# First attention of a two-layer model: single PSUM banks in rings of three, the shift and the value products placed at other steps, loops written out

## The reference

```python
x = x + delta_rule_attention(layernorm(x))     # layer 0
x = x + attention_and_experts(layernorm(x))    # layer 0: 16 heads of width 8, then 8 experts
x = x + attention(layernorm(x))                # layer 1: 32 heads of width 32
x = x + fourier_filter(layernorm(x))           # layer 1
```

```python
q, k, v = hn @ wq + bq, hn @ wk + bk, hn @ wv + bv     # 16 heads of width 8
scores = einsum('bhqd,bhkd->bhqk', q, k) / sqrt(8)
attn = softmax(scores, axis=-1)
o = einsum('bhqk,bhkd->bhqd', attn, v)
x = x + (o @ wo + bo)
```

## Time and profile before

| | us |
|---|---|
| Median of three runs | 2202.83 |
| The runs | 2204.41, 2199.51, 2202.83 |
| The profiled execution | 2194.15 |
| Its span, from the first to the last instruction | 2192.4 |

### The profile page before, as it was taken

How to read it: one execution, slowest core, us unless ns; L and a number is a source line. 1 busy time by engine, 2 the same in 40 slices (tenths; PEclk the granted TensorE clock), 3 DMA queues, 4 the chain that set the end, 5 groups by cost and what they waited for, 6 DMA issues and landing times. The chain is left out here.

```text
span 2192.4 us, 49876 instructions
## 1 busy us (share of the span) xinstructions
PE 1866.6 (85%) x18758; PEld 864.7 (39%) x18758; DVE 1681.2 (77%) x2951; ACT 1244.5 (57%) x2377; POOL 1132.9 (52%) x683
## 2 busy tenths in 40 slices
PE   5457753899999965897998999999999999999975
PEld 3357631122322224573442344444444444444433
DVE  8832565787878728444655999999999999999947
ACT  5312142677777740124773677777777777777755
POOL 8622641000000007331110788888888888888868
PEclk9778766799999985898997999999999999999995
DMA  1220046111111114116777333222323222333201
GB/s 45 48 31 3 0 124 182 35 36 43 35 35 42 29 48 132 47 50 230 285 304 239 79 79 78 70 70 78 79 79 79 74 71 72 79 79 79 64 10 40
DMA packets 198304, 179.84 MB, mean 82 GB/s; under 512 B 59508, under 2 KB 161012, under 8 KB 197892
## 3 DMA queue, kind: packets, MB, share of 16 engines
q1 hardware_dynamic: 189700, 170.02, 27.1%
q0 software_dynamic: 2944, 7.10, 1.1%
q10 hardware_dynamic: 5504, 0.73, 0.2%
HBM read 101.16 MB, written 75.26 MB: 80 GB/s over the span
## 5 line engine op out<-in xcount | busy, mean ns | idle before, releaser
L892 POOL TENSOR_TENSOR part_sums_l<-probs_l 128x1024 f32<-128x1024 f32 x256 | 610.3, 2384 | 214.4 <-ACT probs_l L957 203.9
L957 ACT ACTIVATE probs_l<-exp_l 128x512 f32<-128x512 f32 x1024 | 573.6, 596 | 166.4 <-PE exp_l L1005 148.7
L916 DVE TENSOR_REDUCE maxima_l<-max_l 128x1 f32<-128x512 f32 x1024 | 643.9, 679 | 4.3 <-PE max_l L994 1.5
L994 PE MATMUL max_l<-k_stack_l,q_stack_l 96*128 96x512 f16 x1024 | 400.0, 391 | 12.2 <-DVE pv_bank_l L908 10.3
L1005 PE MATMUL exp_l<-q_stack_l,k_stack_l 100*128 100x512 f16 x1024 | 389.7, 381 | 2.0 <-ACT probs_l L957 1.6
L1210 DVE TENSOR_REDUCE maxima_l<-max_l 128x2 f32<-128x1024 f32 x256 | 305.7, 1223 | 79.7 <-PE max_l L1293 78.4
L1246 ACT ACTIVATE probs_l<-exp_l 128x512 f32<-128x512 f32 x512 | 282.8, 598 | 117.1 <-PE exp_l L1307 116.3
L1039 PE MATMUL pv_bank_l<-probs_l,v_ring_l 128*32 128x512 f32 x2048 | 272.7, 605 | 0.3 <-issue 0.3
L1715 POOL IOTA rows_e<- 128x32 int32 x1 | 0.2, 184 | 455.2 <-POOLq L26 455.2
L994 PEld LDWEIGHTS max_l<-k_stack_l,q_stack_l 96*128 96x128 f16 x1024 | 99.7, 97 | 289.3 <-DVE maxima_l L916 216.7
L898 POOL TENSOR_TENSOR part_sums_l<-part_sums_l 128x512 f32<-128x512 f32 x128 | 184.1, 1438 | 10.0
(11 more groups left out here) (278 smaller groups left out, 2561.2 us busy)
## 6 DMA issues: line engine op xcount, KB each, us to landing
scratch_qk_l<-parts_g SPq DMA_DIRECT2D x128, 256.0 KB, 2.7
q_stack_l<-scratch_qk_l SPq DMA_DIRECT2D x192, 128.0 KB, 2.9
k_stack_l<-scratch_qk_l SPq DMA_DIRECT2D x192, 128.0 KB, 3.0
scratch_v_l<-v_g SPq DMA_DIRECT2D x16, 1024.0 KB
v_ring_l<-scratch_v_l SPq DMA_DIRECT2D x64, 256.0 KB, 3.4
scratch_stack_l<-parts_c SPq DMA_DIRECT2D x96, 128.0 KB, 2.4
q_stack_l<-scratch_stack_l SPq DMA_DIRECT2D x64, 96.0 KB, 2.1
k_stack_l<-scratch_stack_l SPq DMA_DIRECT2D x64, 96.0 KB, 2.1
```

Of the source, the lines that this page charges most:

```text
L892: pool.tensor_tensor(part_sums[:, i, h, :, :], probs[:, i, h, 0:2, :], probs[:, i, h, 2:4, :], ALU.add).then_inc(pair_sum.sem, 1)
L916: dve.reduce_max(maxima[:, s % 2, at % NT, at // NT:at // NT + 1], max_bank(n, at)[:, :], AX).then_inc(max_taken.sem, 1)
L957: act.activation(probs[:, i, at // NT, at % NT, :], exp_ps[at % 2][:, :], ACT.Exp, scale=a.scale).then_inc(prob_tile.sem, 1)
L994: pe.matmul(max_bank(n, at)[:, :], qs[0:SHIFT_ROW, s % RING, h, k * P:(k + 1) * P], ks[0:SHIFT_ROW, s % RING, h, :], start=True, stop=True ...
```

## The change

It touches `attention_l0` alone.

- PSUM: the two pairs `max_ps` become three single banks, and `exp_ps` gets three instead of two. Tile `at` of group `n` uses bank `(n * TILES + at) % 3` in either ring, and PE waits for the tile three before.
- DVE reduces each tile by itself: 16 reductions of 128 x 512 in a group instead of 8 of 128 x 1024.
- ACT makes `shift` after tile 4 instead of tile 6 (`L0_SHIFT_AT`). It copies `pv_bank` after tile 0 instead of tile 1 (`L0_COPY_AT`).
- The pieces of the values move (`L0_VALUES_AT`): two at step 1, one each at 2, 3 and 4, two at step 5, one at 6, none at 7. Before, there was one at each of steps 1 to 7, with two at step 3.
- The loops are gone: every engine's program of this stage is written out, and waits on constants.

The core of the diff:

```diff
-PV_PIECES = {1: (0,), 2: (1,), 3: (2, 3), 4: (4,), 5: (5,), 6: (6,), 7: (7,)}
...
+L0_MAXT_AT, L0_SHIFT_AT, L0_COPY_AT = 2, 4, 0
+L0_VALUES_AT = (1, 1, 2, 3, 4, 5, 5, 6)
+L0_VALUEST_AT, L0_INVERSE_AT = 4, 4
+L0_OT_AT, L0_OUT_AT = 7, 7
...
-        max_ps, exp_ps = [pb(f"max{i}", HALVES, N) for i in range(2)], [pb(f"exp{i}", N) for i in range(HALVES)]
+        max_ps, exp_ps = [pb(f"max{i}", N) for i in range(3)], [pb(f"exp{i}", N) for i in range(3)]
...
+        def bank(n, at):
+
+            return (n * TILES + at) % 3
...
-                        dve.wait_ge(max_pair.sem, max_pair.made(n, p))
-                        dve.reduce_max(maxima[:, s % 2, :, k, hh], max_ps[p % 2][:, :, :], AX).then_inc(max_taken.sem, 1)
...
+                        for half in range(HALVES):
+                            at = HALVES * p + half
+                            dve.wait_ge(max_tile.sem, max_tile.made(n, at))
+                            dve.reduce_max(maxima[:, s % 2, half, k, hh:hh + 1], max_ps[bank(n, at)][:, :], AX).then_inc(max_taken.sem, 1)
...
-                        if at == 6 and exists(turn, s, 1):
+                        if at == L0_COPY_AT and exists(turn, s, OUT_LAG):
+                            act.wait_ge(pv_ps.sem, pv_ps.made(n - OUT_LAG, 0))
+                            if exists(turn, s, OUT_LAG + 1):
+
+                                act.wait_ge(pvT_ps.sem, pvT_ps.made(n - OUT_LAG - 1, 0))
+                            act.copy(pv[:, :], pv_bank[:, :]).then_inc(pv_sb.sem, 1)
+                        if at == L0_SHIFT_AT and exists(turn, s, 1):
...
-                    if p == 0 and exists(turn, s, OUT_LAG):
-                        act.wait_ge(pv_ps.sem, pv_ps.made(n - OUT_LAG, 0))
-                        if exists(turn, s, OUT_LAG + 1):
-
-                            act.wait_ge(pvT_ps.sem, pvT_ps.made(n - OUT_LAG - 1, 0))
-                        act.copy(pv[:, :], pv_bank[:, :]).then_inc(pv_sb.sem, 1)
-
-            stream(act, step)
+
+            for n in range(M + OUT_LAG + 3):
+                step(n // U, n % U)
...
-                        if p >= 2:
-                            pe.wait_ge(max_taken.sem, max_taken.made(n, p - 2))
...
+                            at = HALVES * p + half
+                            if at >= 3:
+                                pe.wait_ge(max_taken.sem, max_taken.made(n, at - 3))
...
-                            if p:
-                                pe.wait_ge(prob_tile.sem, prob_tile.made(m, at - HALVES))
+                            if at >= 3:
+                                pe.wait_ge(prob_tile.sem, prob_tile.made(m, at - 3))
...
-                        for piece in PV_PIECES[p]:
+                        for piece in [piece for piece in range(2 * NT) if L0_VALUES_AT[piece] == p]:
```

## The result

The changed kernel takes 2132.62 us, the median of four runs (2129.23 to 2134.26), against 2201.17 us for the kernel before in the same comparison (2198.28 to 2204.41). The medians lie 68.5 us apart, 3.1%. The ratio of the two kernels is estimated as 0.9695, with a 95% interval from 0.9678 to 0.9713; it is not the quotient of these two medians, which is 0.9689. Between the two profiled executions the difference is 59.9 us (2194.15 to 2134.26). The profiled execution of the kernel before, which all sums are made against, was 7.0 us under its median, that of the changed kernel 1.6 us over its own.

What follows compares the result with a forecast made beforehand. Bound: the PE-ACT-PE-ACT-SP-PE chain over the shift's DMAs. 31 turns of 10.7 (331.7), 4 for `wo` and 14 for the clock make 350 instead of 397 us: 47 off 2202.83 gives 2156, range 2140 to 2184.

Steps and rivals of the forecast that it cites:

- The old bound and the length of the new chain: First exp product through shift and DMAs to the next: 12.02 us before, 10.55 after, 1.47 less; chance as bound 0.60.
- The lag: From the shift's end over SP's eight DMAs to the next first exp product: 6.53 us, unchanged.
- The plain turn: Turn of the first attention's stage without the product by `wo`: 10.7 us, ends 10.3 and 11.6.
- DVE takes over: Rival: reductions at 0.68 us make DVE the bound, 11.6 us a group; 29 us less, 2174; chance 0.16.
- The turn with `wo`: One turn in four, with the product by `wo`: 0.5 us over the plain one; 4 us for eight turns.
- PE takes over: Rival: paired max products no longer run together, 12.2 us of PE a turn; 5 us less, 2198; chance 0.07.
- The clock: PE's clock in the stage: falls stay, ten instead of eighteen assumed, costing 14 us in the sum.
- the two rivals with more falls or a slower clock: Falls in every turn: 20 us less, 2183, chance 0.10. PE at 1.2 GHz throughout: 160 us more, chance 0.05.
- The third exp bank: PE's exp-product waits at steps 0 and 1: zero by itself; without it the copy's 0.48 us could be lost.
- The loops: Writing out the stage's programs: counted as zero; register work at most 0.1 us a turn, 3 us in all.
- The pieces: Value products moved off step 7, leaving it to the product with `wo`; a double piece holds PE 0.98 us.
- The median: Whole kernel's time: 47 us taken off the median of 2202.83, giving 2156.

Runs made afterwards that it cites:

- e4: Changed kernel with the shift back after tile 6 and the copy back after tile 1; 2216.91 us, ratio to the kernel before 1.0085.
- e8: Changed kernel with DVE taking the maximum of only the first 256 of 512 columns of each tile; 2122.06 us, ratio 0.9649.
- e11: Changed kernel with the shift alone back after tile 6, the copy staying after tile 0; 2183.48 us, ratio 0.9925.
- e1: Kernel before with the loops of the first attention written out, nothing else changed; 2195.61 us, ratio 0.9989.
- e2: Kernel before with loops written out, shift after tile 4 and copy after tile 0, banks and pieces as before; 2195.64 us, ratio 0.9991.
- e3: Kernel before with PE making the max products of steps 0 and 1 three times over; 2189.87 us, ratio 0.9959.
- e5: Changed kernel with two banks for the exponentials instead of three; 2201.04 us, ratio 1.0006.
- e7: Kernel before with loops written out, shift and copy sooner and pieces as changed, banks as before; 2203.33 us, ratio 1.0023.
- e12: Kernel before with loops written out, shift and copy sooner, and max products of step 1 made three times over; 2183.41 us, ratio 0.9923.
- e10: Changed kernel measured once more, in another series; 2135.87 us, ratio 0.9712.
- e6: Changed kernel with the pieces of the values placed as before; 2139.55 us, ratio 0.9728.

## Why the prediction was right and wrong

**The old bound and the length of the new chain: right.** Every step from the first exp product to the end of the shift came within 0.15 us of the forecast, the end of the shift within 0.02. e4, e8 and e11, in which this chain is the bound, have turns of its length plus 6.36 to 6.38. The lag I had at 6.53; it is 6.36 to 6.38 in e1 already, so the difference came with the loops, written out on all engines at once. What was wrong is that the cut of the chain would count in full: e2 shows the next limit just behind it.

**The plain turn: right in size (10.7 forecast, 10.74 measured), wrong in what sets it.** I had the DMA chain as the bound at 10.55 and DVE 0.4 us behind. It is DVE, at 10.74, with the chain at 10.38 (e8). DVE's own work is 10.1 us, sixteen reductions 0.60 apart and 0.49 for the division, where I had 10.2. The other 0.66 are lost where PE is late with a max product: 0.28 twice and 0.1 once. I had expected 0.1 to 0.3 us of this, so that the size of 10.7 came out is in part luck. The reductions are 0.60 apart, not 0.68, so the rival "DVE takes over" came true in its mechanism and not at its price. The turn with `wo` is 0.75 over the plain one, where I had 0.5. Without the clock my sum was 335.7 and the stage is 338.45. In the rival "PE takes over" the sum holds a 0.53 that no row gives; with the 0.44 that it names for a pair apart it would be 11.5 us of PE and not 12.2.

**The clock: wrong, and the step that failed.** The prediction says "So falls stay" and sets 14 us for ten of them. There are none from 409 us on, so the term measured zero; nor did the two rivals with more falls or a slower clock come true. With the falls at zero my own sum gives 61 us less, against 59.9 between the profiled executions. I had looked at how long PE is thinly used, and that did not change: from the last piece to piece 0 it is 2.92 us before and 3.01 us now. What changed is how busy PE is in it. Here are the two stretches, the first of the kernel before, the second of the changed one; the first figure behind the length is PE's busy time:

```profile
607.02:609.94 2.92, 1.87 (x12) 0.59 (x9) 2.83 (x3) 2.34 (x6) 0.00 (x0) 1.00 0.44 127
```

```profile
609.08:612.09 3.01, 2.58 (x17) 0.76 (x13) 3.01 (x7) 2.95 (x7) 0.00 (x0) 1.00 0.37 92
```

64% against 86%. In the kernel before, PE stood for 0.41 us waiting for the DMAs, then 0.36 for an exp bank and 0.18 for the copy; in the changed one its longest idle time in this stretch is 0.21 us, for a bank of the maxima. e3 shows that falls go when PE is given work there, and e4 and e11 that they come back when it is made to wait for the DMAs in the changed kernel.

The busy share does not say by itself when a fall comes. This is the same stretch one turn earlier in the kernel before:

```profile
595.00:597.93 2.93, 1.86 (x13) 0.58 (x9) 2.82 (x3) 2.33 (x6) 0.00 (x0) 1.00 0.43 124
```

It is as long and as thin as the one at 607.02, and the clock stayed at 1.00 through the whole turn behind it; behind the other it fell at 610.40.

I also counted eighteen falls from a clock of 0.92 that held the 18 us of the slow start; from 409 us on the clock was 0.94, which is 45 us, or thirteen stretches of 3.4.

**The third exp bank: wrong.** "Zero by itself", and worth 0.48 a turn at most if it were missing. e5 is level with the kernel before: without this bank the whole gain is gone. The error was to see one wait that it removes and not what is queued behind it on PE: the pieces, the next max products and with them DVE and the transposition. I priced the new chain by ACT's rows and took for granted that PE would reach each product in time.

**The loops: right.** 0 forecast, 0.1% measured, at the limit of what can be told. In a plain turn they cost 0.16 us, where I had allowed 0.1.

**The pieces: half right.** Their use lies in the turn with `wo`, as written; in plain turns the double piece costs 0.24.

**The median.** The rest of the miss is in the reference. I took the 47 us off the median of three runs, 2202.83, and came to 2156, 23 us over what was measured. Of these, 13 are the gain that I missed between the profiled executions; 8.7 are the distance of the kernel before's profiled execution from that median, and 1.6 that of the changed kernel's from its own. In the three series that followed, the medians of the kernel before were 2198.29, 2198.05 and 2198.90, and the changed kernel measured again was 63.0 below the last.

What stays open: in which turns a fall comes. It differs between turns with the same stretch, as shown above, and between kernels with the same turns (e5 and e7), and no run here was made to find the condition. Open too is which single wait makes the limit of 11.83 to 11.90 in e2, e5 and e7: the rows of e5 show the second exp product of step 1 standing for tile 1, but e5 takes the third bank away at every step at once.

## What to carry to other kernels

When a loop through several engines sets the period, look for the next loop before pricing a cut: here the second stood no more than 0.2 us behind the first, and neither the cut (e2) nor the bank (with the shift late, e11: 15 us) was worth much without the other. Price a buffer by what stands behind its wait in the in-order program of the engine that waits, not by the wait itself. And when a change gives TensorE work in a stretch where it waited, do not carry the old falls of its clock over into the sum: here 14 us hung on them. That the stretch keeps its length is no reason for them to stay.

## What the runs showed of the hardware

- A fall to 0.50 for 3.4 us made a turn 1.2 to 1.4 us longer in the kernel before (12.03 to between 13.23 and 13.41, 13.10 to between 14.30 and 14.45) and 1.3 to 1.5 longer in plain turns of e4 (12.16 to between 13.64 and 13.69) and e11 (11.66 to between 12.95 and 13.15). So falls can outweigh the length of the turns: e4 has plain turns only 0.14 us longer than the kernel before, but a clock of 0.88 instead of 0.94, and its stage takes 21.5 us more.
- Falls went when TensorE got work in its waits (e3: clock 0.94 to 0.99; e12: 0.92 to 0.97). Two stretches of 2.92 and 2.93 us with 1.87 and 1.86 us of work were followed by a fall in one turn and by none in the other.
- Kernels with falls scatter more. Ten runs of e5 lie between 2190.45 and 2210.81 and ten of e7 between 2196.96 and 2210.16, while five of e10 lie between 2135.05 and 2136.24 and four of e6 between 2137.20 and 2139.83. The changed kernel, with none, has four between 2129.23 and 2134.26. That the falls make the scatter is argued from this, not shown.
- Redundant matmuls made the kernel faster: e3 makes 128 pairs of max products more than the kernel before and is 0.4% quicker; e12 makes 64 more than e2 and has a ratio of 0.9923 to e2's 0.9991.
- Reductions of 128 x 512 from PSUM have a mean length of 682 ns and follow each other every 0.60 us. Those of 128 x 256 (e8) follow every 0.33 to 0.34 us, those of 128 x 1024 (before) every 1.14 us. The cost of one in a row is the distance between starts, not the length shown.
